# Two PSUM banks for the attended rows' transposes and output products, the second norm's two steps in two slots, the first row statistics one slot earlier

## What is computed

```python
h = layernorm(x) * (1 + ca) + sa
x = x + ga * (attention(h) @ w_out + b_out)        # 16 heads, band of 64 rows on either side
h = layernorm(x) * (1 + cb) + sb
x = x + gb * ffn(h)                                # 64 experts, 8 for each row, 256 rows for each expert
```

## Time and profile before

| | us |
|---|---|
| median of 3 runs | 989.44 |
| the runs | 984.01 to 989.56 |
| the profiled execution | 989.2 |
| its span in the trace | 987.5 |

### The profile page before, as it was taken

How to read it: one execution, slowest core, us unless ns; L and a number is a source line. 1 busy time by engine, 2 the same in 40 slices (tenths; PEclk the granted TensorE clock), 3 DMA queues, 4 the chain that set the end, 5 groups by cost and what they waited for, 6 DMA issues and landing times.

```text
span 987.5 us, 15482 instructions
## 1 busy us (share of the span) xinstructions
PE 719.3 (73%) x4732; PEld 470.7 (48%) x4732; DVE 544.6 (55%) x1974; ACT 373.7 (38%) x827; POOL 643.2 (65%) x592
## 2 busy tenths in 40 slices
PE   4579998997997897989988861200899998888200
PEld 3235555554554564554455530200788777666100
DVE  3566569779869878778678772600222222222038
ACT  2135654544444455445444530000344333333100
POOL 5206332687786886886885656776388888887630
PEclk9879998998987998898898976555899999999755
DMA  8695996275466446534526379100999999898878
GB/s 306 162 341 159 333 336 189 82 251 180 172 202 227 151 157 212 181 101 162 172 97 201 115 227 282 37 5 4 247 277 276 263 231 159 162 161 182 216 211 332
DMA packets 165134, 191.60 MB, mean 194 GB/s; under 512 B 21497, under 2 KB 146581, under 8 KB 165052
## 3 DMA queue, kind: packets, MB, share of 16 engines
q1 hardware_dynamic: 128636, 134.27, 42.7%
q0 software_dynamic: 30720, 38.03, 18.8%
q10 hardware_dynamic: 5696, 18.30, 5.2%
HBM read 100.77 MB, written 110.67 MB: 214 GB/s over the span
## 4 chain that ended last, share of the span: by engine, by line
PE 36%; DVE 20%; POOL 15%; DMA 12%; issue 11%; SPq 3%; ACT 2%; POOLq 0%; DVEq 0%; ACTq 0%
POOL acc_d L725 8%; DMA acc_d<-ys,xg 7%; PE stageA L952 6%; POOL slots_d L642 5%; PE outT L1022 4%; PE scores L980 4%; PE scoresT L1181 4%; DVE junk L1249 4%; PE scoresT L1002 4%; PE scoresT L1006 3%; PE stageA L962 2%; DVE pairs L1313 2%; PE stageC L1077 2%; DVE sc L1313 1%; PE stageC L1059 1%
## 5 line engine op out<-in xcount | busy, mean ns | idle before, releaser
L642 POOL DMA_INDIRECT slots_d<-H,dest x256 | 259.1, 1012 | 95.0 <-issue 57.4
L725 POOL DMA_INDIRECT acc_d<-ys,xg x128 | 198.4, 1550 | 60.3 <-issue 29.8
L1249 DVE CUSTOM_DVE_ANT_0 junk<-scores,mask 128x256 bf16<-128x256 f32 x512 | 187.6, 419 | 76.1 <-PE scores L980 75.8
L779 ACT ACTIVATE PT<-scoresT 128x512 f32<-128x512 f32 (+1 forms) x320 | 152.8, 508 | 140.7 <-PE scoresT L1006 137.1
L1181 PE MATMUL scoresT<-xgT,wgu 128*128 128x256 f32 x512 | 127.6, 393 | 23.0 <-ACT xgT L873 22.8
L1002 PE MATMUL scoresT<-mask,identb 128*128 128x512 bf16 (+1 forms) x320 | 116.5, 364 | 19.8 <-DMA Qs<-MT 14.3
L980 PE MATMUL scores<-Ks,Qs 96*128 96x256 bf16 x512 | 108.5, 298 | 30.4 <-DVE mrowmax L1249 26.6
L1181 PEld LDWEIGHTS scoresT<-xgT,wgu 128*128 128x128 f32 x512 | 96.1, 194 | 48.3 <-ACT xgT L873 35.3
L1006 PE MATMUL scoresT<-Qs,Ks 98*128 98x256 bf16 (+1 forms) x640 | 117.1, 267 | 0.0
L1022 PE MATMUL outT<-PT,Va 128*32 128x256 f32 (+1 forms) x1280 | 94.9, 370 | 0.0
L596 POOL TENSOR_TENSOR r<-p,parts 128x512 f32<-128x512 f32 x32 | 39.3, 1227 | 78.7 <-ACT parts L771 77.2
(11 more groups left out here) (195 smaller groups left out, 1179.5 us busy)
## 6 DMA issues: line engine op xcount, KB each, us to landing
xg<-slots_d SPq DMA_DIRECT2D x64, 324.0 KB, 4.4
slots_d<-blank ACTq DMA_DIRECT2D x26, 648.0 KB, 5.1
parts_d<-parts SPq DMA_DIRECT2D x32, 384.0 KB, 2.7
Qs<-parts_d SPq DMA_DIRECT2D x96, 128.0 KB
Ks<-parts_d SPq DMA_DIRECT2D x90, 128.0 KB
acc_d<-zero SPq DMA_DIRECT2D x32, 272.0 KB
wgu<-L_ffn_w_gate_dram SPq DMA_DIRECT2D x64, 128.0 KB, 3.2
wgu<-L_ffn_w_up_dram SPq DMA_DIRECT2D x64, 128.0 KB, 3.3
```

The source lines that it names most:

```text
L642: pool.indirect_dma_start(out=slots_d[:, :], in_=H2[bt.par][:, t, :], in_offset=None, out_offset=bass.IndirectOffsetOnAxis(ap=dest[bt.par] ...
L725: pool.indirect_dma_start(out=acc_d[ACC[e]][:, :], in_=ys[e % NY][:, h, :], in_offset=None, out_offset=bass.IndirectOffsetOnAxis(ap=xg[e % ...
L779: sc_.activation(PT[m % NPT][:, :, 0:w], src, ACT.Exp).then_inc(sems["exp"], 1)
L1249: ins = v.tensor_tensor_reduce(out=junk[:, i, :], in0=bS[n % 2][:, i * 2 * P:(i + 1) * 2 * P], in1=mask[:, edge, :], scale=1.0, scalar=TAK ...
```

## The change

Five things change. (1) The two transposes of `on` go to banks bC and bA and both stand in slot 2. (2) The two output products go to bC and bA and both stand in slot 3 (before 4 and 5); x1 stands in slots 3 and 4, the statistics of x1 in slots 4 and 5. (3) The waits are rewritten: no product waits for `t1` within the pair; the projection of slot 7 waits until the second half's product has been read out of bA. (4) `norm2` stands in slots 7 and 8 (before both in 7). (5) `stats` of half 0 stands in slot 8 of the round (before 9). The last batch's remainder, after the rounds, keeps its banks and its order.

```diff
-    load_x=(-14,), stats=(-11, -10), a_rstd=(-9,), a_norm=(-6,), a_mod=(-9,), hT=(-4, -3), proj=(-2, -1, 7, 8),
+    load_x=(-14,), stats=(-12, -10), a_rstd=(-9,), a_norm=(-6,), a_mod=(-9,), hT=(-4, -3), proj=(-2, -1, 7, 8),
-    xb=(2,), onT=(2, 3), op=(4, 5), x1=(4, 5), x1_store=(10,), xs=(11,), stats2=(5, 5), c_rstd=(5,), xhat=(6,), norm2=(7, 7),
+    xb=(2,), onT=(2, 2), op=(3, 3), x1=(3, 4), x1_store=(10,), xs=(11,), stats2=(4, 5), c_rstd=(5,), xhat=(6,), norm2=(7, 8),
+        PAIR = (bC, bA)
...
-                        c_onT(prev, k)
+                        c_onT(prev, k, PAIR[k])
...
+                if j == 2 and bt.b >= 2:
+                    after(pe, "t1", batch(bt.b - 2), 2)
...
-                if bank is bC and k == 0:
+                if bt.b < B - 1 and bank is bC:
                     after(pe, "key", bt, -1)
-                elif bank is bC:
-                    after(pe, "onT", bt, k)
+                elif bt.b < B - 2:
+                    after(pe, "p32", batch(bt.b + 2), 2)
+                elif bt.b == B - 2:
+                    after(pe, "v", batch(B), 0)
...
-                if bank is bC:
-                    after(pe, "t1", bt, n)
...
-                        c_op(prev, n)
+                        c_op(prev, n, PAIR[n])
...
-                        c_x1(prev, n)
+                        c_x1(prev, n, PAIR[n])
```

## The result

The changed kernel takes 1023.54 us (median of 4 runs, 1022.64 to 1030.87) against 986.73 us for the kernel before (4 runs, 983.3 to 989.56): a ratio of 1.0395, 95% interval 1.0339 to 1.0451. The forecast was 1029 us in a range of 1012 to 1038. The profiled execution is the slowest of the four, 1030.87 us, with a span of 1029.1 us; that of the kernel before was 989.2 and 987.5. The spans differ by 41.6 us, the medians by 36.8.

The account below looks back on a forecast made before the run. The prediction took hand-overs between engines to bound the attention rounds. To 989.2 us it added 28.3 for the wait for x, 10.0 for TensorE's clock and 1.3 for round 6: 1028.8, say 1029 us, range 1012 to 1038.

Parts of the forecast that it names:

- The wait for x: Slot 8, rounds 1 to 5: VectorE waits 6 to 7 us for x, delaying the sum TensorE needs; 28.3 us altogether.
- S: Time when x lands at VectorE, taken to stay as before; in round 5 the issue plus 6.1 us, 424.25.
- S + 2.65: Predicted start of slot 9: x's landing plus 0.88 statistics, 1.24 sum, 0.1 hand-over, 0.43 transposes; 28.3 us over rounds 1 to 5.
- the sum's 1.24 us: VectorE's second-norm sum in slot 8, behind the statistics of x, taken as half of a 2.48 us pair.
- The clock: TensorE at half clock after slot 8's gap: two stretches, 2.0 us a round, 10 us in all, bounds 0 to 17.
- Nothing given back: After slot 9, later slots were to recover none of the shift; bound 1 us a round.
- The pairing: Paired transposes and products: x1's later statistics cost 1.3 us in round 6 (bounds 0 and 2), hidden in rounds 2 to 5.
- Round 7: GpSimd waits 4.15 us for the statistics; VectorE could win some tenths (bounds 0 and 1), taken as 0.

Follow-up runs that it names:

- x early alone: Changed kernel with the load of x issued in slot 4, ahead of the twelve reloads, not slot 6: 1022.17 us, ratio 1.0136 to the kernel before.
- the gap filled: Changed kernel with products of no use on TensorE in slot 8, rounds 1 to 5: 1019.27 us, against 1026.91 us for the changed kernel on that chip.
- xb early: Changed kernel with x loaded in slot 4 and GpSimd's xb steps in slot 1, not 2: 1007.87 us, ratio 1.0001 to the kernel before.
- both numbers: Kernel before with x's first statistics in slot 8 and the second norm's sum in slot 8 behind them: 1023.44 us, ratio 1.0359.

## Why the prediction was right, and where its terms were off

**The wait for x** was the forecast's main step, and it held: VectorE waits in rounds 1 to 5, TensorE's transposes of H are released by VectorE, rounds 6 and 7 have no such slot 8, and x is issued 26.7 us after the start of round 4 (374.33 − 347.6), as before (349.65 − 323.0). VectorE's waits are 5.5, 3.7, 5.9, 4.9 and 2.6 us, not 6 to 7, since the product came later. For the same reason slot 8 lasts 9.7, 6.0, 9.2, 7.1 and 6.1 us, not 8 to 10, and TensorE idles in it for 5.2, 2.0, 4.8, 2.7 and 2.1 us where the forecast had a gap of some 7. S, counted from the round's start, is within 1 us of the forecast in rounds 1 to 4; in round 5 it is 1.5 us earlier, as x landed 4.5 us after its issue and not 6.1.

**S + 2.65**, from x's landing S to slot 9's first product, was mis-sized. It gave 28.3 us over five rounds; 32.0 were measured. The term that failed most is the sum's 1.24 us. The statistics of round 1, the sums of rounds 1, 2 and 5, and GpSimd's work beside these sums (timeline of the changed kernel):

```profile
148.31 0.75 DVE L1217 BATCH_NORM_STATS2 stats<-xt 128x6 f32<-128x256 f32 x2 [5.52 <-DMA xt<-L_attn_x_dram]
...
149.12 1.15 POOL L601 TENSOR_TENSOR parts<-p,parts 128x512 bf16<-128x512 f32 x1
149.19 2.15 DVE L1307 TENSOR_TENSOR H<-H,mr 128x1024 f32<-128x1024 f32 x1
...
225.21 1.16 POOL L601 TENSOR_TENSOR parts<-p,parts 128x512 bf16<-128x512 f32 x1
225.23 2.23 DVE L1307 TENSOR_TENSOR H<-H,mr 128x1024 f32<-128x1024 f32 x1
...
456.34 1.18 POOL L598 TENSOR_TENSOR r<-p,parts 128x512 f32<-128x512 f32 x1
456.41 3.31 DVE L1307 TENSOR_TENSOR H<-H,mr 128x1024 f32<-128x1024 f32 x1
457.46 1.17 POOL L601 TENSOR_TENSOR parts<-p,parts 128x512 bf16<-128x512 f32 x1
```

The sum takes 2.15, 2.23, 1.31, 1.19 and 3.31 us, 10.2 in all where 6.2 were counted. In its old place it took 1.22 us beside an indirect store (rounds 2 to 6); now it starts while GpSimd is splitting. In rounds 1, 2 and 5 the splitting steps end at 150.27, 226.37 and 458.63, and the sum ends 1.07, 1.09 and 1.09 us later, about its own length: it was held until they were done. In round 1 of the run with x early alone the order is the other way: the sum starts 0.22 us ahead of a splitting step and takes 1.19 us, and that step takes 1.99 and not 1.17. By the Trainium skill, page "SBUF — State Buffer", section "Who interferes with whom", a VectorE instruction with two SBUF inputs contends with a GpSimd instruction that reads SBUF. These sums agree.

The sum gives 4.0 us over the forecast. Another 1.4 us come between the sum's end and slot 9: 0.97 us in rounds 1, 3 and 4, in which the transposes already ran at a lowered clock, where 0.53 were counted. S took 1.7 us back, 1.5 of them in round 5. Together that is the difference of 3.7.

**The clock** was forecast at 10.0 us over five rounds. Slots 9 and 10 lost 9.7; the run with the gap filled says 7.6 for the time as a whole. The size held, with some luck. Two stretches of 0.92 are 1.8 us a round, which the forecast rounded up to 2.0; and the gap was shorter than it said: TensorE idled for 2.0 to 5.2 us in slot 8 and not 7, and the clock fell even so, also after the shortest of these gaps (slots 9 and 10 of round 2 lost 1.6 us). **Nothing given back** did not quite hold: slots 11 to 19 are 5.7 us shorter in rounds 1 to 5, just past the bound of 1 us a round. The runs show that it goes with the lowered clock and the gap (with the statistics back in slot 9 these rounds gave back nothing in sum), but not which wait shrinks; that stays open.

**The pairing** was forecast to lose 1.3 us in round 6 and to be hidden in rounds 2 to 5. The wait for xb is there:

```profile
359.87 0.69 DVE L1285 TENSOR_TENSOR x<-stageC,mr 128x512 f32<-128x512 f32 x1 [4.23 <-POOL xc L615]
360.60 2.06 DVE L1288 TENSOR_TENSOR x<-x,xc 128x512 f32<-128x512 f32 x1
...
368.23 0.30 DVE L1298 BATCH_NORM_AGGREGATE mv<-stats 128x2 f32<-128x6 f32 x2
368.62 0.23 POOL L627 TENSOR_SCALAR ve<-mv 128x4 f32<-128x4 f32 x1 [1.12 <-DVE mv L1298]
```

GpSimd's step (round 4) comes 21.0 us after the round's start, where it came after 20.0. The working had +1.3; so it held for this step. But the slots up to 7 grew by 1.3 to 4.3 us in rounds 1 to 5: TensorE's gaps in slots 5 and 6 lower its clock too. Busy time by stretch in the changed kernel, where slot 6 starts at 364.8 and slot 8 at 376.3:

```profile
361.40:364.80 3.40, 1.73 (x23) 0.92 (x20) 3.37 (x11) 0.77 (x2) 2.93 (x3) 1.00 0.68 237
364.80:368.20 3.40, 2.16 (x13) 1.36 (x10) 3.40 (x15) 1.19 (x2) 2.09 (x2) 0.51 0.99 342
368.20:371.60 3.40, 3.40 (x21) 1.63 (x20) 2.42 (x13) 1.49 (x3) 2.56 (x5) 0.50 0.98 313
371.60:375.00 3.40, 3.40 (x16) 1.26 (x15) 2.59 (x11) 2.14 (x5) 2.49 (x4) 0.50 0.88 268
```

TensorE is busy for half of the first stretch, and slots 6 and 7 then run at the 1.2 GHz level, back at full clock by slot 8. With xb early the granted clock of slot 6 is 0.78 to 1.00 in rounds 2 to 6; with x early alone, on the same chip, it is 0.52 to 0.64. In round 6 it was 2.1 us and not 1.3. That these losses would be swallowed by the wait for x as long as they are below it was right: slot 8 grew by 18.8 us in rounds 1 to 5, not by 28.3, and slot 9's start moved by the wait for x and what follows it alone. The kernel with both numbers and nothing of the pairing shows it: its slots 0 to 8 in rounds 1 to 5 are 33.1 us longer than before, with the pairing 32.0. **Round 7** lost 2.3 us, not 0. Nothing was run for it.

That the total came out right is partly luck. In the trace, 3.7 us too little for the wait and 4.3 too little for rounds 6, 7 and the start met 5.7 us given back that the forecast's total did not have; of the 4.3, the start's 1.3 is noise. And the trace is of the slowest of the four executions: its span grew by 41.6 us and the median by 36.8, on either side of the 39.6 that were forecast.

## What to carry to other kernels

In a list that an engine works through in order, a step that waits for a transfer must not stand ahead of one that others wait for, unless the landing is early. Moving the statistics one slot earlier cost 1.1%, moving the sum to the next slot nothing, and both together 3.6%. Read for each wait when what it waits for lands (issue plus time to landing), and who is queued behind. A start that moves earlier only helps up to the next in-order list: here x1's products were ready and xb, one slot too late on GpSimd, held them.

## What the runs showed of the hardware

TensorE's clock behind a gap of 2.1 to 6.6 us cost 1.6 to 2.6 us a round, and products without use in the gap took that back: 7.6 us of 1027 by the medians. A VectorE addition of 1.22 us took up to 3.31 us when it started during one of GpSimd's splitting steps, and ended some 1.1 us after these. The kernel before took 988.6, 1007.0 and 987.8 us on the three chips of the experiments; on the second, slot 16 of the kernel before with x early lasted up to 7.5 us where it took 4 to 5, for a cause that was not looked into.
